# Quantising `w_down` and part of `w_gate` between the steps of attention instead of after it

## The chip, the cores and the metric

One Trainium2 chip, all 8 of its cores. Each core runs the same program on one of the 8 sequences of the batch; no core talks to another. The metric is the device time of the slowest core, in microseconds.

## The reference

One transformer layer in post-norm form, on `x` of 8 x 2048 x 1024. Attention has 16 heads of width 64, and its scores are multiplied by a decay in the distance of the two positions. The feed-forward part quantises its activations and all three weights to FP4 values in blocks of 16 along the last dimension.

```python
scores = einsum('bqhd,bkhd->bhqk', q, k) * scale
scores = scores * exp(-alpha * |i - j|)
attn   = softmax(scores)
x = layernorm(x + (attn @ v) @ Wo.T + bo)

def fp4_quant_dequant(x):            # blocks of 16
    scale = max(max(|xb|) / 6, 1e-12)
    xn = xb / scale
    return GRID[searchsorted(MID, |xn|)] * sign(xn) * scale
def fp4_linear(x, w): return fp4_quant_dequant(x) @ fp4_quant_dequant(w).T

h = silu(fp4_linear(x, w_gate)) * fp4_linear(x, w_up)    # w_gate, w_up: 2816 x 1024
x = layernorm(x + fp4_linear(h, w_down))                 # w_down: 1024 x 2816
```

## The kernel before

There is no scheduler. `Prog` keeps one list of instructions for each engine, filled in the order in which the Python code is run, and each engine works through its own list strictly in that order. `wait` puts a semaphore wait in front of what follows, `do` adds an instruction that raises a semaphore, and `chain` adds one that also waits for everything its own engine has done so far. VectorE raises `sV`, TensorE `sT`, ScalarE `sA`; loads by the SyncE queue raise `dS`.

The work of a core runs in these stages, one after the other:

1. `x` is loaded and transposed, and Q, K and V are projected.
2. **Attention** (the loop at L413). The 8 pairs of heads and 4 blocks of 512 queries make 32 units, and each unit has 16 steps `kt`, one for each 128 keys: 512 steps in all. In a step TensorE computes the scores of both heads of the pair into `ps_s1` and `ps_s2` (L423; two buffers each, so TensorE can be two steps ahead of VectorE), and then, for the same `kt` of the unit before, the products with V and the row sums into `ps_av` and `ps_d` (L397, L404). VectorE multiplies the scores by the decay table `Wd` with two 128x512 instructions (L449), into the ring `SDr1`/`SDr2`. It waits there for all that TensorE was given in this step. After every fourth step ScalarE takes the exponential of the four steps' scores for each head (L461) and writes `PT1`/`PT2`. The ring holds 12 steps, three groups of four. At the end of a unit ScalarE turns the row sums into reciprocals (`recD`, L477 and L479), and VectorE multiplies `ps_av` by them (L484). TensorE's products of the next unit wait for that.
3. The output projection, the residual sum and the first layer norm, whose result goes to `x1_dram`.
4. The normed activations are loaded, quantised and transposed into `x1qT`, in 8 slices.
5. **`w_down`** (loop at L664): 8 rows of 128x2816 are loaded to `wst`, quantised into `wqo`, and stored to `wdq_dram`.
6. **`w_gate` and `w_up`** (loop at L684): 11 chunks each, of 2 rows of 128x1024. A chunk is loaded, quantised, and transposed on TensorE through `emit_pe_tp` (L209: eight groups of two transposes, each evacuated by a VectorE copy, L219) into `wgT` or `wuT`.
7. Gate, up, SiLU and the quantising of `h`, for 16 tiles of tokens; `h` is transposed by DMA and stored.
8. `wdq_dram` is loaded and transposed, and the down projection, the residual sum and the last layer norm follow.

`quant_stages` (L125) quantises a tile in two halves, and each half in three stages. `front` has six VectorE instructions: the maximum of each block (L150), the scale (L153), its reciprocal (L156), the normed values (L157), and two roundings (L159, L165). `mid` has two, a comparison (L172) and a predicated copy (L177). `back` has four (L182, L184, L187, L188). That is 12 for a half and 24 for a tile, all on VectorE and all chained. ScalarE adds a square in `front` (L163) and one in `mid` (L175) for each half.

Of the kernel before, what the change touches and what calls it, by code (L numbers as in the profile page):

```python
# [6 lines left out]
F32 = mybir.dt.float32  # L7
# [8 lines left out]
D = 1024  # L16
# [43 lines left out]
def build_program(debug=False):  # L60
# [17 lines left out]
    wdq_dram = nc.dram_tensor("wdq_scr", [D, I_FF], BF16, kind="Internal").ap()  # L78
    hqT_dram = nc.dram_tensor("hqT_scr", [NTT, 128, I_FF], BF16, kind="Internal").ap()
# [11 lines left out]
    with ExitStack() as es:  # L91
# [29 lines left out]
        junk_t = es.enter_context(nc.sbuf_tensor("junk_t", [128, 256], BF16))  # L121
# [129 lines left out]
        with nc.sbuf_tensor("QT", [128, NCT * T], BF16) as QT, \  # L251
# [121 lines left out]
            with nc.sbuf_tensor("SDr1", [128, 12 * 512], F32) as SDr1, \  # L373
                 nc.sbuf_tensor("SDr2", [128, 12 * 512], F32) as SDr2, \
# [8 lines left out]
                p.wait("tensor", sA, sA_proj)  # L383
                wd_stride = 3968
                units = [(hp, qc) for hp in range(NP) for qc in range(NQC)]
                sd_kt = {0: 0, 1: 0}
                exp_ring = {0: 0, 1: 0, 2: 0}
# [25 lines left out]
                for u in range(len(units) + 1):  # L413
                    if u < len(units):
                        hp, qc = units[u]
                        for kt in range(NTT):
                            b2 = kt % 2
                            r8 = (kt // 4) % 3
# [24 lines left out]
                            s8 = kt % 12  # L443
# [11 lines left out]
                            if kt % 4 == 3:  # L455
# [10 lines left out]
                                exps_grp[(u, g)] = sA.n  # L466
                    if u >= 1:
# [19 lines left out]
                        evac_done[up] = sV.n  # L487
            sV_attn = sV.n
# [123 lines left out]
        if True:  # L612
# [41 lines left out]
            with nc.sbuf_tensor("wgT", [128, NCT * I_FF], BF16) as wgT, \  # L654
# [4 lines left out]
                with nc.sbuf_tensor("wst", [128, 2 * I_FF], F32) as wst, \  # L659
                     nc.sbuf_tensor("wqo", [128, 2 * I_FF], BF16) as wqo:  # L660
                    wd_r = wd_h.rearrange("(r p) i -> p r i", p=128)
                    wdq_r = wdq_dram.rearrange("(r p) i -> p r i", p=128)
                    q_end = {0: 0, 1: 0}
                    for rt in range(8):  # L664
                        par = rt % 2
                        p.wait("sync", sV, q_end[par])
                        p.wait("sync", dS, dS.n)
                        p.do("sync", lambda e, rt=rt, par=par: e.dma_start(
                            out=wst.ap()[:, par * I_FF:(par + 1) * I_FF],
                            in_=wd_r[:, rt, :]), dS, 16)  # L670
                        p.wait("vector", dS, dS.n)
                        p.wait("vector", dWQ[par])
                        emit_quant(wst.ap()[:, par * I_FF:(par + 1) * I_FF], I_FF, qb,
                                   wqo.ap()[:, par * I_FF:(par + 1) * I_FF])
                        q_end[par] = sV.n
                        p.wait("gpsimd", sV, sV.n)
                        p.do("gpsimd", lambda e, rt=rt, par=par: e.dma_start(
                            out=wdq_r[:, rt, :], in_=wqo.ap()[:, par * I_FF:(par + 1) * I_FF]), dWQ[par], 16)
# [5 lines left out]
                    for w_src, wTa, dbgk in ((wg_h, wgTa, "d_wgq"), (wu_h, wuTa, None)):  # L684
                        w_r = w_src.rearrange("(r p) c -> p r c", p=128)
                        for ch in range(11):
                            par = cidx % 2
                            cidx += 1
                            p.wait("sync", sV, q_end[par])
                            p.wait("sync", dS, dS.n)  # L690
                            p.do("sync", lambda e, ch=ch, w_r=w_r, par=par: e.dma_start(
                                out=wst.ap()[:, par * I_FF:par * I_FF + 2 * D].rearrange(
                                    "p (r c) -> p r c", c=D),
                                in_=w_r[:, 2 * ch:2 * ch + 2, :]), dS, 16)
                            p.wait("vector", dS, dS.n)
                            p.wait("vector", sT, wqo_reads[par])
                            p.wait("vector", dWQ[0])
                            p.wait("vector", dWQ[1])
                            wqop = wqo.ap()[:, par * I_FF:par * I_FF + 2 * D]
                            emit_quant(wst.ap()[:, par * I_FF:par * I_FF + 2 * D], 2 * D, qb, wqop)  # L700
# [252 lines left out]
```

How the kernel before makes its waits and increments, by code:

```python
    def wait(self, eng, sem, val=None):  # L42
        v = sem.n if val is None else val
        if v <= 0:
            return
        self.ops[eng].append(lambda e, s=sem.h, v=v: e.wait_ge(s, v))
# [1 line left out]
    def do(self, eng, fn, sem=None, k=1):  # L48
        if sem is not None:
            sem.n += k
            self.ops[eng].append(lambda e, f=fn, s=sem.h, kk=k: f(e).then_inc(s, kk))
        else:
            self.ops[eng].append(fn)
```

## Time and profile before

| what | us |
|---|---|
| median of the timed runs (3241.70 to 3243.77) | 3242.74 |
| the profiled execution's own time | 3252.38 |
| its span on the slowest core (core 2) | 3250.8 |
| spans of the eight cores | 3230.2 to 3250.8 |
| VectorE busy (share of the span) | 2194.5 (68%) |
| TensorE matmuls busy | 1452.6 (45%) |
| ScalarE busy | 969.1 (30%) |

The span is the time from the first to the last instruction on one core; about 1.6 us of the profiled execution lie around it. The profiled execution was some 10 us longer than the median. A busy share is taken over the whole program, whose stages are bound by different things, so it doesn't tell which engine sets the time of a stage; the stages have to be read one by one.

### The profile page before, as it was taken

The page shows a single profiled execution, that of the slowest core. Times are in us where ns is not written, and L with a number is a line of the kernel's source. Part 1 is how long each engine was busy: PE and PEld are TensorE (multiplying, and loading weights), DVE is VectorE, ACT ScalarE, POOL GpSimd, SP SyncE. Part 2 cuts the span into 40 slices and gives each one's busy share as a digit, 9 for nine tenths or more (in the row PEclk, how much of TensorE's full clock was granted, in tenths as well). Part 3 has the DMA queues.
Part 4 walks back from the last instruction along what each step waited for, and adds up shares of the span by engine and source line. Part 5 has one row for each costly group of instructions (what it writes and reads, how often), then busy time and mean ns, then how long its engine had stood idle before and what let it go on. Part 6 is the DMA issues. An engine that isn't in the chain of part 4 may idle for free.

```text
span 3250.8 us, 25238 instructions; the slowest of 8 cores (3230.2 to 3250.8 us)
## 1 busy us (share of the span) xinstructions
PE 1452.6 (45%) x7186; PEld 540.4 (17%) x7186; DVE 2194.5 (68%) x2968; ACT 969.1 (30%) x844; POOL 23.1 (1%) x37
## 2 busy tenths in 40 slices
PE   5777655556555557100000000000046666663298
PEld 2332111111111112000000000000022222221243
DVE  2004766777666754688899788888868888888233
ACT  1214555555555544211112111111112222222022
POOL 0000000000000000000000000000000000000000
PEclk9888888888888878555555555555568888887599
DMA  5110000000000015210222111111100111111344
GB/s 78 26 26 1 1 1 1 1 1 1 1 1 1 1 27 161 84 39 26 81 61 75 48 39 39 39 39 39 39 1 22 39 38 46 39 39 39 115 176 157
DMA packets 88473, 136.95 MB, mean 42 GB/s; under 512 B 59154, under 2 KB 59154, under 8 KB 87314
## 3 DMA queue, kind: packets, MB, share of 16 engines
q1 hardware_dynamic: 73986, 88.66, 9.2%
q0 software_dynamic: 9744, 29.89, 3.9%
q10 hardware_dynamic: 4608, 16.78, 1.3%
q8 instruction: 62, 1.02, 0.1%
q14 instruction: 73, 0.60, 0.1%
HBM read 102.25 MB, written 34.08 MB: 42 GB/s over the span
## 4 chain that ended last, share of the span: by engine, by line
DVE 46%; PE 19%; ACT 16%; issue 11%; DMA 6%; DVEq 1%; SPq 1%; ACTq 0%; POOL 0%; POOLq 0%
ACT PT L461 12%; DVE SDr L449 6%; PE ps_o L850 5%; DVE qc L187 5%; DVE qxn L157 5%; DVE qr L150 5%; PE ps_q L327 4%; DVE qc L177 3%; DVE qm L182 3%; DVE qc L159 3%; DVE qc L184 3%; DVE wqo L188 2%; DVE qm L172 2%; DVE qr L156 2%; PE ps_av L397 2%
## 5 line engine op out<-in xcount | busy, mean ns | idle before, releaser
L449 DVE TENSOR_TENSOR SDr<-ps_s,Wd 128x512 f32<-128x512 f32 x1024 | 640.4, 684 | 311.1 <-PE ps_s L423 220.8
L461 ACT ACTIVATE PT<-SDr 128x2048 bf16<-128x2048 f32 x256 | 474.9, 1902 | 402.9 <-DVE SDr L449 402.9
L163 ACT ACTIVATE qcc<-qc 128x1024 bf16<-128x1024 bf16 (+1 forms) x108 | 129.5, 1199 | 1144.8 <-DVE qc L159 1144.8
L215 PE MATMUL ps_tp<-idn,wqo 128*128 128x128 bf16 x352 | 52.6, 291 | 803.7 <-DVE wqo L188 781.9
L397 PE MATMUL ps_av<-PT,VV 128*64 128x512 bf16 x1024 | 236.1, 453 | 222.4 <-DVE QT L484 222.4
L744 PE MATMUL ps_g<-wgT,x1qT 128*128 128x512 bf16 (+1 forms) x768 | 212.4, 430 | 182.7 <-DVE hbuf L763 182.0
L423 PE MATMUL ps_s<-QT,KT 64*128 64x512 bf16 x1024 | 221.8, 421 | 157.4 <-DVE SDr L449 152.5
L404 PE MATMUL ps_d<-PT,ones 128*64 128x512 bf16 x1024 | 226.9, 434 | 0.0
L750 PE MATMUL ps_u<-wuT,x1qT 128*128 128x512 bf16 (+1 forms) x768 | 185.2, 388 | 0.0
L175 ACT ACTIVATE qcc<-qc 128x1024 bf16<-128x1024 bf16 (+1 forms) x108 | 129.5, 1199 | 125.9 <-DVE qm L172 125.9
L215 PEld LDWEIGHTS ps_tp<-idn,wqo 128*128 128x128 bf16 x352 | 25.7, 108 | 830.5 <-issue 826.0
L187 DVE COPY_PREDICATED qc<-qm,qc 128x1024 bf16<-128x1024 int8 (+1 forms) x108 | 151.9, 1406 | 11.1
L177 DVE COPY_PREDICATED qc<-qm,qc 128x1024 bf16<-128x1024 int8 (+1 forms) x108 | 151.8, 1406 | 11.1
L850 PE MATMUL ps_o<-wdT,hin 128*128 128x512 bf16 x704 | 154.1, 382 | 3.3 <-DMA x1in<-x_scr 3.3
L484 DVE TENSOR_TENSOR QT<-ps_av,recD 128x512 bf16<-128x512 f32 x32 | 22.1, 692 | 179.2 <-ACT recD L479 179.2
L423 PEld LDWEIGHTS ps_s<-QT,KT 64*128 64x128 bf16 x1024 | 63.4, 94 | 429.7 <-issue 429.7
L744 PEld LDWEIGHTS ps_g<-wgT,x1qT 128*128 128x128 bf16 x768 | 77.8, 108 | 303.3 <-issue 260.5
L327 PE MATMUL ps_q<-XT,wbuf 128*128 128x512 bf16 x512 | 115.1, 389 | 18.5 <-DMA wbuf<-wkT 17.8
L397 PEld LDWEIGHTS ps_av<-PT,VV 128*64 128x64 bf16 x1024 | 61.4, 111 | 355.8 <-issue 354.8
L215 PE MATMUL ps_tp<-idn,x1q 128*128 128x128 bf16 x128 | 18.8, 291 | 219.2 <-DVE x1q L188 211.3
L763 DVE TENSOR_TENSOR hbuf<-sg,ps_u 128x512 f32<-128x512 f32 x96 | 61.5, 641 | 68.4 <-ACT sg L757 68.4
L750 PEld LDWEIGHTS ps_u<-wuT,x1qT 128*128 128x128 bf16 x768 | 81.3, 106 | 98.7 <-issue 38.6
(95 smaller groups left out, 1901.1 us busy)
## 6 DMA issues: line engine op xcount, KB each, us to landing
wst<-wd SPq DMA_DIRECT2D x8, 1408.0 KB
wst<-wg SPq DMA_DIRECT2D x11, 1024.0 KB
wst<-wu SPq DMA_DIRECT2D x11, 1024.0 KB
hqT_scr<-hqT POOLq DMA_DIRECT2D x16, 704.0 KB, 3.4
hin<-hqT_scr SPq DMA_DIRECT2D x16, 704.0 KB
xres<-x SPq DMA_DIRECT2D x16, 512.0 KB, 4.5
x_scr<-ra ACTq DMA_DIRECT2D x16, 512.0 KB, 2.7
x1sl<-x_scr SPq DMA_DIRECT2D x8, 1024.0 KB
```

The costliest lines, as they stand in the source:

```text
L150: C(lambda e, d=d: e.tensor_reduce(out=d["r"], in_=d["src3"], axis=AX.X, op=ALU.max, apply_absolute_value=True))
L177: C(lambda e, d=d: e.copy_predicated(out=d["c1"], mask=d["m"], data=d["c2"]))
L187: C(lambda e, d=d: e.copy_predicated(out=d["c1"], mask=d["m"], data=d["c2"]))
L327: p.do("tensor", lambda e, i=i, j=j, q4=q4, g=g: e.matmul(out=psq[:, g, q4 * 512:(q4 + 1) * 512], lhsT=wba[:, i, j * 128:(j + 1) * 128], r ...
L397: p.do("tensor", lambda e, kt=kt, PT=PT, rq0=rq0, h=h: e.matmul(out=ps_av.ap()[rq0:rq0 + 64, :], lhsT=VVa[:, kt, h * 64:(h + 1) * 64], rhs ...
L404: p.do("tensor", lambda e, kt=kt, PT=PT, rq0=rq0: e.matmul(out=ps_d.ap()[rq0:rq0 + 64, :], lhsT=ones64[:, :], rhs=PT.ap()[:, kt * QC:(kt + ...
L423: e.matmul(out=ps.ap()[:, b2 * 512:b2 * 512 + QC], lhsT=KTa[rq0:rq0 + 64, hp, kt * 128:(kt + 1) * 128], rhs=QTa[rq0:rq0 + 64, hp, qc * QC: ...
L449: return e.tensor_tensor(out=SDr.ap()[:, s8 * 512:(s8 + 1) * 512], in0=ps.ap()[:, b2 * 512:b2 * 512 + QC], in1=wd_ap, op=ALU.mult)
L461: e.activation(out=PT.ap()[:, 4 * g * QC:(4 * g + 4) * QC], in_=SDr.ap()[:, r8 * 2048:(r8 + 1) * 2048], func=AF.Exp), sA, 1)
L744: e.matmul(out=ps_g.ap()[:, g * 512:g * 512 + ilen], lhsT=x1qTa[:, i, tt * 128:(tt + 1) * 128], rhs=wgTa[:, i, i0:i0 + ilen], start=(i == ...
L750: e.matmul(out=ps_u.ap()[:, g * 512:g * 512 + ilen], lhsT=x1qTa[:, i, tt * 128:(tt + 1) * 128], rhs=wuTa[:, i, i0:i0 + ilen], start=(i == ...
L850: p.do("tensor", lambda e, it=it, c=c, g=g, hin3=hin3: e.matmul(out=pso[:, g, c * 512:(c + 1) * 512], lhsT=hin3[:, it, :], rhs=wdTa[:, it, ...
```

## The change

The same quantising of `w_down`, and of the first 8 of the 22 rows of `w_gate`, is recorded inside the loop over the attention steps. It is cut into 24 chunks: 16 half rows of `w_down` (128x1408) and 8 rows of `w_gate` (128x1024). Each chunk owns 21 steps in a row; its load, six quantising stages and store come behind the VectorE work of steps 0, 2, 4, 6, 8, 10, 12 and 13 of the 21. A half of a chunk is thus 704 or 512 columns wide. New buffers of their own (`awst`, `awq` and the `aq...` tiles) hold the work, and to make room for them the ring of scores goes from 12 steps to 8. The quantised rows of `w_gate` go to a new scratch `wgq_dram`. Stage 5 is gone; in stage 6 the first four chunks of `w_gate` are loaded from `wgq_dram` straight into `wqo` and only transposed, and the other 18 chunks are as before.

```diff
+    wgq_dram = nc.dram_tensor("wgq_scr", [I_FF, D], BF16, kind="Internal").ap()
...
-            with nc.sbuf_tensor("SDr1", [128, 12 * 512], F32) as SDr1, \
-                 nc.sbuf_tensor("SDr2", [128, 12 * 512], F32) as SDr2, \
+            with nc.sbuf_tensor("SDr1", [128, 8 * 512], F32) as SDr1, \
+                 nc.sbuf_tensor("SDr2", [128, 8 * 512], F32) as SDr2, \
...
+                for rt in range(8):
+                    for hf in range(2):
+                        aw_chunks.append((wd_r2[:, rt, hf * 1408:(hf + 1) * 1408],
+                                          wdq_r2[:, rt, hf * 1408:(hf + 1) * 1408],
+                                          1408))
+                for row in range(8):
+                    aw_chunks.append((wg_r2[:, row, :], wgq_r2[:, row, :], 1024))
...
+                def aw_actions(k):
+                    src, dst, Fk = aw_chunks[k]
+                    stg = quant_stages(awst.ap()[:, :Fk], Fk, aqb, awq.ap()[:, :Fk])
+                    def a_load():
+                        if k >= 1:
+                            p.wait("sync", sV, aw_read[k - 1])
+                        p.wait("sync", dS, dS.n)
+                        p.do("sync", lambda e, src=src, Fk=Fk: e.dma_start(
+                            out=awst.ap()[:, :Fk], in_=src), dS, 16)
+                        aw_load[k] = dS.n
+                    def a_f0():
+                        p.wait("vector", dS, aw_load[k])
+                        stg[0]()
+                    def a_f1():
+                        stg[1]()
+                        aw_read[k] = sV.n
+                    def a_b0():
+                        if k >= 1:
+                            p.wait("vector", dWQ[0], aw_store[k - 1])
+                        stg[4]()
+                    def a_store():
+                        p.wait("gpsimd", sV, sV.n)
+                        p.do("gpsimd", lambda e, dst=dst, Fk=Fk: e.dma_start(
+                            out=dst, in_=awq.ap()[:, :Fk]), dWQ[0], 16)
+                        aw_store[k] = dWQ[0].n
+                    return [a_load, a_f0, a_f1, stg[2], stg[3], a_b0, stg[5],
+                            a_store]
+                for k in range(len(aw_chunks)):
+                    acts = aw_actions(k)
+                    base = k * 21
+                    for oi, off in enumerate((0, 2, 4, 6, 8, 10, 12, 13)):
+                        aw_sched[base + off] = acts[oi]
...
-                            r8 = (kt // 4) % 3
+                            r8 = (kt // 4) % 2
...
-                            s8 = kt % 12
+                            s8 = kt % 8
...
                                 exps_grp[(u, g)] = sA.n
+                            act = aw_sched.get(u * NTT + kt)
+                            if act is not None:
+                                act()
...
-                    for rt in range(8):
...
-                        emit_quant(wst.ap()[:, par * I_FF:(par + 1) * I_FF], I_FF, qb,
-                                   wqo.ap()[:, par * I_FF:(par + 1) * I_FF])
...
+                    for w_src, wTa, preq, dbgk in ((wg_h, wgTa, 4, "d_wgq"),
+                                                   (wu_h, wuTa, 0, None)):
...
+                            if ch < preq:
+                                p.wait("sync", sT, wqo_reads[par])
+                                p.wait("sync", dS, dS.n)
+                                p.do("sync", lambda e, ch=ch, wq3=wq3: e.dma_start(
+                                    out=wq3, in_=wgq_r[:, 2 * ch:2 * ch + 2, :]), dS, 16)
+                                p.wait("tensor", dS, dS.n)
+                            else:
...
```

**VectorE's list, the end of the first unit that has a normalisation.** `SDr` is the scaled scores, `QT` the normed output of the unit before, `aqm`, `aqc`, `aqs` and `awq` the new quantising tiles. Before:

```order
L449 TENSOR_TENSOR SDr<-ps_s,Wd 128x512 [waits sT,sA]
L449 TENSOR_TENSOR SDr<-ps_s,Wd 128x512
L484 TENSOR_TENSOR QT<-ps_av,recD 128x512 [waits sA,sT]
L449 TENSOR_TENSOR SDr<-ps_s,Wd 128x512 [waits sT,sA]
L449 TENSOR_TENSOR SDr<-ps_s,Wd 128x512
```

and now (the line numbers are those of the changed kernel):

```order
L524 TENSOR_TENSOR SDr<-ps_s,Wd 128x512 [waits sT,sA]
L524 TENSOR_TENSOR SDr<-ps_s,Wd 128x512
L183 TENSOR_SCALAR aqm<-aqcc 128x704 [waits dWQa,sA,sV]
L185 TENSOR_SCALAR aqc<-aqxn 128x704 [waits sV]
L188 COPY_PREDICATED aqc<-aqm,aqc 128x704 [waits sV]
L189 TENSOR_TENSOR awq<-aqc,aqs 128x704 [waits sV]
L562 TENSOR_TENSOR QT<-ps_av,recD 128x512 [waits sA,sT]
L524 TENSOR_TENSOR SDr<-ps_s,Wd 128x512 [waits sT,sA]
L524 TENSOR_TENSOR SDr<-ps_s,Wd 128x512
```

Here a `back` stage falls on step 15, between the last scores of the unit and the instruction that waits for `recD`.

**VectorE's list, inside a unit.** Two steps that stood next to each other before,

```order
L449 TENSOR_TENSOR SDr<-ps_s,Wd 128x512 [waits sT]
L449 TENSOR_TENSOR SDr<-ps_s,Wd 128x512
L449 TENSOR_TENSOR SDr<-ps_s,Wd 128x512 [waits sT]
L449 TENSOR_TENSOR SDr<-ps_s,Wd 128x512
```

now have a `front` stage between them; the first one of all also waits for the load (`dS`):

```order
L524 TENSOR_TENSOR SDr<-ps_s,Wd 128x512 [waits sT]
L524 TENSOR_TENSOR SDr<-ps_s,Wd 128x512
L151 TENSOR_REDUCE aqr<-awst 128x44 [waits dS,sV]
L154 TENSOR_SCALAR aqs<-aqr 128x44 [waits sV]
L157 RECIPROCAL aqr<-aqs 128x44 [waits sV]
L158 TENSOR_TENSOR aqxn<-awst,aqr 128x704 [waits sV]
L160 TENSOR_SCALAR aqc<-aqxn 128x704 [waits sV]
L166 TENSOR_SCALAR aqc<-aqxn 128x704 [waits sV]
L524 TENSOR_TENSOR SDr<-ps_s,Wd 128x512 [waits sT]
L524 TENSOR_TENSOR SDr<-ps_s,Wd 128x512
```

The next scores can't start until the six instructions are done.

**SyncE's queue behind the loads of the activations.** Before it held the loads of `wd`, `wg` and `wu`:

```order
L668 DMA wst<-wd 128x2816 [waits sV,dS]
L668 DMA wst<-wd 128x2816 [waits dS]
L668 DMA wst<-wd 128x2816 [waits sV,dS] x6
L691 DMA wst<-wg 128x2x1024 [waits sV,dS] x11
L691 DMA wst<-wu 128x2x1024 [waits sV,dS] x11
```

and now:

```order
L759 DMA wqo<-wgq_scr 128x2x1024 [waits sV,dWQa,dS]
L759 DMA wqo<-wgq_scr 128x2x1024 [waits dS]
L759 DMA wqo<-wgq_scr 128x2x1024 [waits sT,dS] x2
L765 DMA wst<-wg 128x2x1024 [waits dS] x2
L765 DMA wst<-wg 128x2x1024 [waits sV,dS] x5
L765 DMA wst<-wu 128x2x1024 [waits sV,dS] x11
```

Eight loads of `wd` have gone and four of the eleven chunks of `wg` come from the scratch; each load still waits for the one before it (`dS`).

## Rows read from the trace of the kernel before

**Rows 1.** Page part 2: busy tenths and granted clock, slices of 81.3 us

```profile
DVE  2004766777666754688899788888868888888233
...
PEclk9888888888888878555555555555568888887599
```

**Rows 2.** By stage: PE, PEld, DVE, ACT, POOL busy, clock, DMA, GB/s

```profile
274.89:1207.50 932.61, 551.85 (x3070) 144.94 (x3068) 662.40 (x1056) 514.15 (x320) 0.00 (x0) 0.82 0.00 1
...
1549.90:1804.66 254.76, 0.00 (x0) 0.00 (x0) 216.11 (x193) 44.05 (x32) 4.30 (x8) 0.50 0.24 76
1804.66:2404.80 600.14, 51.95 (x348) 25.45 (x348) 499.73 (x701) 93.02 (x88) 0.00 (x0) 0.50 0.10 35
```

**Rows 3.** VectorE's waits in the attention stage: us, times, longest

```profile
DVE QT L484 <- ACT recD L479: 179.2, 32, 10.4
DVE SDr L449 <- PE ps_d L404: 69.1, 107, 1.6
DVE SDr L449 <- ACT PT L461: 4.4, 2, 4.0
```

**Rows 4.** Timeline at a unit boundary: start, duration, instruction, idle before

```profile
699.50 1.89 ACT L461 ACTIVATE PT<-SDr 128x2048 bf16<-128x2048 f32 x1
701.48 0.60 ACT L477 ACTIVATE recD<-ps_d 128x512 f32<-128x512 f32 x1
...
702.97 0.69 DVE L484 TENSOR_TENSOR QT<-ps_av,recD 128x512 bf16<-128x512 f32 x1 [5.44 <-ACT recD L479]
...
705.16 1.29 DVE L449 TENSOR_TENSOR SDr<-ps_s,Wd 128x512 f32<-128x512 f32 x2 [1.50 <-PE ps_d L404]
...
706.71 1.29 DVE L449 TENSOR_TENSOR SDr<-ps_s,Wd 128x512 f32<-128x512 f32 x2 [0.26 <-PE ps_d L404]
...
708.75 17.91 DVE L449 TENSOR_TENSOR SDr<-ps_s,Wd 128x512 f32<-128x512 f32 x28 [0.75 <-PE ps_s L423]
```

**Rows 5.** TensorE, two short stretches there: length, busy, clock, DMA

```profile
704.80:705.60 0.80, 0.80 (x6) 0.50 0.00 0
710.40:711.20 0.80, 0.73 (x6) 1.00 0.00 0
```

**Rows 6.** Groups by shape: busy us, mean ns of one, idle before

```profile
L187 DVE COPY_PREDICATED qc<-qm,qc 128x1408 bf16<-128x1408 int8 x48 | 78.1, 1628 | 4.9
...
L187 DVE COPY_PREDICATED qc<-qm,qc 128x1024 bf16<-128x1024 int8 x60 | 73.7, 1228 | 6.2
...
L163 ACT ACTIVATE qcc<-qc 128x1408 bf16<-128x1408 bf16 x48 | 66.1, 1377 | 496.9 <-DVE qc L159 496.9
...
L157 DVE TENSOR_TENSOR qxn<-wst,qr 128x1024 f32<-128x1024 f32 x44 | 53.9, 1226 | 5.0 <-DVE qr L156 0.5
...
L159 DVE TENSOR_SCALAR qc<-qxn 128x1408 bf16<-128x1408 f32 x48 | 42.9, 894 | 5.1
...
L159 DVE TENSOR_SCALAR qc<-qxn 128x1024 bf16<-128x1024 f32 x60 | 41.6, 694 | 6.4
...
L156 DVE RECIPROCAL qr<-qs 128x88 f32<-128x88 f32 x48 | 33.7, 703 | 5.0
L156 DVE RECIPROCAL qr<-qs 128x64 f32<-128x64 f32 x60 | 33.2, 553 | 6.2
...
L157 DVE TENSOR_TENSOR qxn<-wst,qr 128x1408 f32<-128x1408 f32 x16 | 26.0, 1626 | 1.7
...
L153 DVE TENSOR_SCALAR qs<-qr 128x64 f32<-128x64 f32 x60 | 11.7, 195 | 6.7 <-DVE qr L150 0.5
```

**Rows 7.** Timeline: first instructions of two successive rows of `wd`

```profile
1557.36 1.62 DVE L150 TENSOR_REDUCE qr<-wst 128x88 f32<-128x1408 f32 x1 [7.46 <-DMA wst<-wd]
...
1586.89 1.62 DVE L150 TENSOR_REDUCE qr<-wst 128x88 f32<-128x1408 f32 x1
```

**Rows 8.** Chain that ended last: two loads (start us, us)

```profile
1326.29 5.68 DMA x1sl<-x_scr
...
3047.30 4.41 DMA wdq_sb<-wdq_scr
```

More of the change, by code:

```diff
@@ L120, in build_program @@
         small = es.enter_context(nc.sbuf_tensor("small", [128, 16], F32))
-        junk_t = es.enter_context(nc.sbuf_tensor("junk_t", [128, 256], BF16))
+        junk_t = es.enter_context(nc.sbuf_tensor("junk_t", [128, 16], BF16))
         idn = es.enter_context(nc.sbuf_tensor("idn", [128, 128], BF16))
@@ L383, in build_program @@
                 p.wait("tensor", sA, sA_proj)
+                aq_es = ExitStack()
+                aq_sb = lambda n, sh, dt: aq_es.enter_context(nc.sbuf_tensor(n, sh, dt))
+                awst = aq_sb("awst", [128, 1408], F32)
+                awq = aq_sb("awq", [128, 1408], BF16)
+                aqxn = aq_sb("aqxn", [128, 1408], F32)
+                aqc1 = aq_sb("aqc1", [128, 1408], BF16)
+                aqc2 = aq_sb("aqc2", [128, 1408], BF16)
+                aqcc = aq_sb("aqcc", [128, 1408], BF16)
@@ new lines, in build_program @@
+                aqm = aq_sb("aqm", [128, 1408], I8)
+                aqr = aq_sb("aqr", [128, 88], F32)
+                aqs = aq_sb("aqs", [128, 88], F32)
+                aqb = {"r": aqr.ap(), "s": aqs.ap(), "xn": aqxn.ap(),
+                       "c1": aqc1.ap(), "c2": aqc2.ap(), "cc": aqcc.ap(),
+                       "m": aqm.ap()}
+                wd_r2 = wd_h.rearrange("(r p) i -> p r i", p=128)
+                wdq_r2 = wdq_dram.rearrange("(r p) i -> p r i", p=128)
+                wg_r2 = wg_h.rearrange("(r p) c -> p r c", p=128)
@@ new lines, in build_program @@
+                aw_load = {}
+                aw_read = {}
+                aw_store = {}
+                p.wait("sync", dG, dG.n)
+                p.wait("sync", sT, sT.n)
+                p.wait("sync", sV, sV.n)
+                aw_sched = {}
+                def aw_actions(k):
[25 more added lines that the diff above has]
+                            a_store]
@@ L660, in build_program @@
                      nc.sbuf_tensor("wqo", [128, 2 * I_FF], BF16) as wqo:
-                    wd_r = wd_h.rearrange("(r p) i -> p r i", p=128)
-                    wdq_r = wdq_dram.rearrange("(r p) i -> p r i", p=128)
+                    p.wait("sync", dWQ[0])
                     q_end = {0: 0, 1: 0}
-                    for rt in range(8):
[L665 to L672, printed above, removed]
-                        emit_quant(wst.ap()[:, par * I_FF:(par + 1) * I_FF], I_FF, qb,
-                                   wqo.ap()[:, par * I_FF:(par + 1) * I_FF])
[L675 to L678, printed above, removed]
                     cidx = 0
@@ L683, in build_program @@
                     wT_done = 0
-                    for w_src, wTa, dbgk in ((wg_h, wgTa, "d_wgq"), (wu_h, wuTa, None)):
+                    wgq_r = wgq_dram.rearrange("(r p) c -> p r c", p=128)
+                    for w_src, wTa, preq, dbgk in ((wg_h, wgTa, 4, "d_wgq"),
+                                                   (wu_h, wuTa, 0, None)):
                         w_r = w_src.rearrange("(r p) c -> p r c", p=128)
@@ L688, in build_program @@
                             cidx += 1
[L689 to L695, printed above, removed]
@@ L709, in build_program @@
                                 p.wait("gpsimd", sV, sV.n)
+                                p.wait("gpsimd", dS, dS.n)
                                 p.do("gpsimd", lambda e, ch=ch, dbgk=dbgk, wq3=wq3: e.dma_start(
```

23 lines of the change are left out of this document (16 added, 7 removed).

## The prediction

> **What bounds the kernel now.** I read the views in this order: the slices of the page, the same times by stage, VectorE's waits in attention, the timeline of one unit boundary, and the groups of instructions by shape.
>
> The slices show VectorE at 6 to 9 tenths in most of the program, and TensorE's granted clock at half (5 tenths) from slice 17 to 29, where it has little to do [rows 1]. By stage, the quantising of `w_down` takes 254.8 us with 216.1 us of VectorE work and no matmul at all, and the stage of `w_gate` and `w_up` takes 600.1 us with 499.7 us of VectorE work [rows 2]. The gaps there are the short pauses between chained instructions, so both stages are bound by VectorE. Attention takes 932.6 us with 662.4 us of VectorE work [rows 2]: VectorE idles for 270 us of it, which looks like room for work from elsewhere.
>
> The waits tell where this room lies. 179.2 us are one wait in each of 32 units, for `recD`; 69.1 us are waits for TensorE before a score [rows 3]. The timeline shows the shape of it: behind the last scores ScalarE does two exponentials (1.89 us the one shown), 0.60 us and as much again for the reciprocal, and VectorE idles 5.44 us; then it idles 1.50 us for TensorE, and after two steps it runs 28 score instructions in 17.91 us, one step in 1.28 us, with no gap [rows 4]. So in 13 or 14 of a unit's 16 steps VectorE is the bound itself, and work put between these steps is paid in full.
>
> **What the new instructions cost.** The trace has them at halves of 1408 and 1024 columns [rows 6]. Three of the twelve run like L157 (1626 and 1226 ns; the maximum and the last product are of that kind), two are predicated copies (1628 and 1228), five are like L159 (894 and 694), one is the reciprocal (703 and 553), and L153 takes 0.2 us. A half is 3 x 1.626 + 2 x 1.628 + 5 x 0.894 + 0.703 + 0.2 = 13.51 us at 1408 columns and 10.35 us at 1024: 8.23 ns a column, and some 1.9 us that don't depend on the width. On that line a half of 704 columns takes 7.72 us and one of 512 takes 6.14 us. The pauses come on top: two rows of `w_down` start 29.53 us apart [rows 7], of which 2 x 13.51 = 27.02 are work; 2.5 us for 24 instructions, 0.105 us each. A chunk of `w_down` then costs 15.44 + 2.5 = 17.94 us, 16 of them 287 us, and one of `w_gate` 12.28 + 2.5 = 14.78 us, 8 of them 118 us. **Added: 405 us**, because halves half as wide pay the fixed part twice as often: `w_down` alone took 8 x 29.53 = 236 us before.
>
> The pauses are a place where the Trainium skill says otherwise. "VectorE: DVE Perf Modes", section "The DRAIN you can't avoid", has it that the semaphore between chained instructions costs nothing extra. By this rule the 24 chunks would cost 405 - 60 = 345 us. The rows speak against it: the 2.5 us in 29.53 are there where nothing else runs, and score instructions with no wait between them follow each other at 0.64 us.
>
> **What of it is hidden.** Counting 21 x k + offset over the 24 chunks, 9 of the 144 quantising stages fall on a step 15, in front of the wait for `recD`: 2 `front`, 3 `mid`, 4 `back`. At 704 columns a `front` is 4.1 us, a `mid` 1.6, a `back` 3.3 (the pieces above with their pauses); at 512 a `mid` is 1.3 and a `back` 2.7. A `back` is hidden whole by the 5.44 us: 2 x 3.3 + 2 x 2.7 = 12 us. `front` and `mid` also put a square into ScalarE's list ahead of the reciprocal; 1.377 us at 1408 columns [rows 6], so 0.7 to 0.9 here, which delays `recD` by 0.8 to 0.9. What stays hidden is 2 x 3.2 + 2 x 0.7 + 0.5 = 8 us. **Hidden: 20 us.** The ring of two groups does no harm: a pair of exponentials takes 3.8 us, and VectorE fills a group in four steps, 5.1 us or more, before it needs that pair's space. It even takes away the 4.4 us in which the second unit waited for the exponential of the first one's last group [rows 3]: **4 us saved**.
>
> **TensorE's clock.** After the idle time at a unit's end the granted clock is 0.50, which is 1.2 GHz, and later in the unit 1.00, 2.4 GHz [rows 5]. At the low level a step is paced by TensorE, at 706.71 - 705.16 = 1.55 us instead of 1.28 [rows 4]. Taking 31 first waits of 1.50 us from the 69.1 leaves 22.6 us, which is what cold steps cost now. In the changed kernel TensorE idles behind each quantising stage, so I expect it at 1.2 GHz there. That costs nothing while stages follow every second step: two steps and the shortest stage take 2.56 + 1.3 = 3.9 us of VectorE and 3.1 to 3.3 us of a cold TensorE. Eleven steps follow the last stage of a chunk without one; TensorE is ahead by two, and nine run free; as at a unit's start I take 0.7 us (22.6 / 32) for each of 24 chunks, 17 us, and drop half of the old 22.6, since about half of the unit starts lie between stages. **Net 6 us lost**, with bounds of -22 (never cold outside) and +50 (all 24 x 9 free steps cold, 216 x 0.33 = 71 us, less 22).
>
> Loads are not in the way: the load of a chunk may start when `front` of the one before is done, some 17 steps ahead, and the DMA engines are idle in attention (0.00 [rows 2]). The stores on POOL's queue have nothing behind them until attention ends. `junk_t` has no part in it.
>
> **Attention in all:** 405 - 20 - 4 + 6 = **387 us longer**.
>
> **What goes.** From 1549.9 to 2404.8 us, 854.9 us lie between the activations' last transpose and the gate matmuls [rows 2]. Instead of that: four loads of 512 KB, each behind the one before. A load of 704 KB took 4.41 us and one of 1024 KB 5.68 [rows 8], so I take 4.3 us each, 17.2 us; the bounds are 3 and 5.7, thus -5 and +6 us. The eight transpose groups of a chunk (about 4 us) fit beside the next load. Then the first `wst` load shows, about 6 us. Then 18 chunks at 600.14 / 22 = 27.28 us [rows 2], 491 us. Sum 514 us, so **341 us are saved**. The three later stages have the same instructions as before.
>
> **Sum:** 387 - 341 = +46 us. The profiled execution took 3252.4 us, so it would be 3298; its distance to the median of the timed runs, some 10 us, isn't the change's, and 3242.7 + 46 = **3289 us**, 1.4% more. Two per cent, about what a measurement of this kernel can tell from no change, is 65 us, so 3178 to 3308 counts as the same.
>
> **Rivals.**
> - *A cold TensorE takes over as the bound (slower).* If its clock stays at 1.2 GHz through all of attention, the free steps are paced by it and the clock term is +50 instead of +6: 3289 + 44 = 3333 us. It decides if more than about 60 of the 216 free steps beyond those in the sum are cold (19 / 0.33). For it: the low clock at each unit's start, and the average of 0.82. Against it: at the low clock TensorE is busy for nearly all of a free step (0.80 of 0.80 [rows 5]), and in this kernel it came back to 2.4 GHz within three such steps. The Trainium skill ("TensorE: Matmul & The Clock Gate", section "HAM oscillation") names this pattern: bursts of matmuls parted by waits each start cold again.
> - *VectorE waits for ScalarE (slower).* A `mid` needs the square of the `front` four steps before, and that square may stand behind a pair of exponentials (3.8 us) that itself waits for TensorE. If each `mid` lost 0.6 us, 48 x 0.6 = 29 us: 3318 us. Against: four steps last 5.1 us without the stages.
> - *The stage's idle time takes the work (faster).* If VectorE's 270 us in attention could be filled but for the 46.5 us at unit starts, 224 us would be hidden: 405 - 224 - 341, some -160 us, 3083 us. For it: the busy share of 71%. Against it: 135 of the 144 stages don't stand in front of the long wait, and VectorE works in order.
> - *The pauses vanish in attention (same).* 60 us less: 3229 us.
>
> **How the numbers follow.** Forecast 0.69, cold TensorE 0.12, ScalarE 0.09, idle time filled 0.04, no pauses 0.06. The forecast's own spread (the clock's bounds, the loads, 0.02 us on 576 pauses is 12 us) puts about 0.10 of its 0.69 above 3308. Slower by over 2%: 0.10 + 0.12 + 0.06 of ScalarE's = 0.28. Faster by over 2%: 0.04. Same: 0.68. The range leaves out the filled idle time and the far ends of the rest: 3245 to 3332 us.
>
> **What would show it.** Right: attention about 1320 us long in the windows, with VectorE busy some 1007 us (662 + 345 of instructions without their pauses); the wait for `recD` down from 179 to about 160 us; chunks of `w_down` whose instructions last 0.89 us (L158) and 0.53 us (L160); gate matmuls some 46 us later than before; hardly any wait for the DMA of `awst`. Wrong: attention much shorter than 1290 us would mean that the stages were hidden; over 1350 us with waits for `ps_d` of 100 us or more would mean a cold TensorE; waits of `aqm` for `aqcc` on ScalarE would be the second rival; a stage of four passes much over 23 us would mean that the loads were mis-sized.

## The result and the profile after

The changed kernel took 3273.18 us (median of 20 runs) against 3246.02 us for the kernel before (median of 19): a ratio of 1.0088, with a 95% interval of 1.0060 to 1.0117. That is 0.9% slower, 27 us between the two medians, within the 2% that count as no change. The forecast was 3289 us, with a range of 3245 to 3332 and a chance of 0.68 for "the same".

The profiled execution took 3296.77 us, with a span of 3295.2 us on core 7. Two cores of it, 6 and 7, came out of the projections 25 to 35 us late at a lower clock (0.76 instead of 0.92 over the same 210 us), which no other core shows. That lies in front of the change, and run 2 below, which has the projections and attention of the kernel before, shows the same on two of its cores; so everything below is read stage by stage.

First the page's busy tenths and granted clock after the change:

```profile
DVE  2002877777777777777358878888877888888323
...
PEclk9777557676666666666785555555559889887599
```

They are the counterpart of [rows 1]: VectorE is at 7 tenths from the third slice of attention to its end, where it went between 6 and 7 before, and the clock there has come down from 8 to 5, 6 and 7.

The stages, in the columns of [rows 2]: attention, the activations' quantising, the four chunks that are only transposed, and the other 18 chunks of weights.

```profile
307.72:1609.90 1302.18, 678.45 (x3070) 152.66 (x3068) 997.06 (x1632) 585.20 (x416) 13.02 (x24) 0.65 0.05 19
...
1724.30:1948.70 224.40, 18.70 (x128) 9.39 (x128) 181.59 (x256) 33.84 (x32) 0.00 (x0) 0.50 0.11 38
1948.70:1969.50 20.80, 9.57 (x64) 4.47 (x64) 8.53 (x33) 0.00 (x0) 0.00 (x0) 0.50 0.46 152
1969.50:2458.50 489.00, 42.19 (x288) 21.06 (x288) 408.28 (x575) 76.13 (x72) 0.00 (x0) 0.50 0.11 37
```

Attention takes 1302.2 us instead of 932.6, 369.6 more. Behind the activations, 20.8 + 489.0 = 509.8 us stand in the place of 854.9, 345.1 less. The two leave 24.5 us, and the medians of the runs show 27.

VectorE's waits in attention, the counterpart of [rows 3]:

```profile
DVE QT L562 <- ACT recD L557: 158.8, 32, 10.6
DVE SDr L524 <- PE ps_d L479: 76.8, 108, 1.6
...
DVE SDr L524 <- ACT PT L536: 1.3, 4, 0.4
```

The wait for `recD` has lost 20.4 us, the waits for TensorE have gained 7.7, and the wait for the exponentials is down by 3.1 us. So VectorE's idle time in attention has hardly been touched: the work went on top. The timeline shows how. Between steps (start, duration, instruction, idle time before it):

```profile
735.02 2.48 DVE L524 TENSOR_TENSOR SDr<-ps_s,Wd 128x512 f32<-128x512 f32 x4 [0.39 <-issue]
...
737.61 0.89 DVE L151 TENSOR_REDUCE aqr<-awst 128x44 f32<-128x704 f32 x1
...
741.05 0.53 DVE L166 TENSOR_SCALAR aqc<-aqxn 128x704 bf16<-128x704 f32 x1
...
741.50 2.47 DVE L524 TENSOR_TENSOR SDr<-ps_s,Wd 128x512 f32<-128x512 f32 x4
...
744.07 0.89 DVE L151 TENSOR_REDUCE aqr<-awst 128x44 f32<-128x704 f32 x1
```

and at a unit's end, with ScalarE's two instructions for `recD`:

```profile
717.59 0.89 DVE L189 TENSOR_TENSOR awq<-aqc,aqs 128x704 bf16<-128x704 bf16 x1
719.17 0.60 ACT L555 ACTIVATE recD<-ps_d 128x512 f32<-128x512 f32 x1
719.86 0.63 ACT L557 ACTIVATE recD<-recD 128x512 f32<-128x512 f32 x1
720.66 0.69 DVE L562 TENSOR_TENSOR QT<-ps_av,recD 128x512 bf16<-128x512 f32 x1 [2.18 <-ACT recD L557]
```

Two steps of scores end at 737.50, a `front` stage of a 704-column half fills VectorE until 741.58, and two more steps follow: the stage has moved them by 4.00 us, all of it paid. At the unit's end a `back` stage ends at 718.48, inside the wait, which is 2.18 us long instead of 5.44 [rows 4]; that one was hidden.

The new shapes in the groups by shape:

```profile
L178 DVE COPY_PREDICATED aqc<-aqm,aqc 128x704 bf16<-128x704 int8 x32 | 28.6, 895 | 3.3
...
L158 DVE TENSOR_TENSOR aqxn<-awst,aqr 128x704 f32<-128x704 f32 x32 | 28.5, 892 | 3.3
...
L160 DVE TENSOR_SCALAR aqc<-aqxn 128x704 bf16<-128x704 f32 x32 | 16.9, 527 | 3.4
```

They are what the straight line through the two widths of [rows 6] gives for 704 columns: 0.89 to 0.90 us and 0.53.

### The profile page after: what moved, and what is told of

It is laid out like the page before. It is cut to its first block, busy times and chain, and to the rows that moved or that the text cites. A ratio compares the mean times of both kernels' runs of the same rounds, so it can differ in the third digit from the quotient of the medians.

```text
span 3295.2 us, 26073 instructions; the slowest of 8 cores (3258.1 to 3295.2 us)
## 1 busy us (share of the span) xinstructions
PE 1601.8 (49%) x7186; PEld 553.1 (17%) x7186; DVE 2228.5 (68%) x3256; ACT 979.6 (30%) x892; POOL 31.3 (1%) x53
## 4 chain that ended last, share of the span: by engine, by line
DVE 50%; PE 20%; issue 14%; ACT 8%; DMA 5%; DVEq 1%; SPq 1%; ACTq 0%; POOL 0%; POOLq 0%
DVE SDr L524 13%; ACT PT L536 5%; PE ps_o L922 5%; PE ps_q L328 4%; DVE qc L188 4%; DVE qxn L158 4%; DVE qr L151 4%; PE ps_q L348 2%; PE ps_av L472 2%; DVE qc L178 2%; PE ps_tp L216 2%; DVE qc L185 2%; DVE qm L183 2%; DVE qc L160 2%; DVE qm L173 2%
## 5 line engine op out<-in xcount | busy, mean ns | idle before, releaser
L498 PE MATMUL ps_s<-QT,KT 64*128 64x512 bf16 x1024 | 269.1, 514 | 377.7 <-DVE SDr L524 372.1
L472 PE MATMUL ps_av<-PT,VV 128*64 128x512 bf16 x1024 | 281.1, 541 | 245.0 <-DVE QT L562 245.0
L164 ACT ACTIVATE qcc<-qc 128x1024 bf16<-128x1024 bf16 (+1 forms) x84 | 99.1, 1179 | 882.0 <-DVE qc L160 882.0
L479 PE MATMUL ps_d<-PT,ones 128*64 128x512 bf16 x1024 | 276.1, 530 | 0.0
L822 PE MATMUL ps_u<-wuT,x1qT 128*128 128x512 bf16 (+1 forms) x768 | 177.5, 376 | 0.0
L328 PE MATMUL ps_q<-XT,wbuf 128*128 128x512 bf16 x512 | 138.3, 445 | 16.7 <-DMA wbuf<-wkT 16.0
L562 DVE TENSOR_TENSOR QT<-ps_av,recD 128x512 bf16<-128x512 f32 x32 | 22.1, 691 | 158.8 <-ACT recD L557 158.8
L176 ACT ACTIVATE qcc<-qc 128x1024 bf16<-128x1024 bf16 (+1 forms) x84 | 99.1, 1179 | 102.1 <-DVE qm L173 102.1
L178 DVE COPY_PREDICATED qc<-qm,qc 128x1024 bf16<-128x1024 int8 (+1 forms) x84 | 115.9, 1380 | 9.0 <-DVE qm L173 0.5
L188 DVE COPY_PREDICATED qc<-qm,qc 128x1024 bf16<-128x1024 int8 (+1 forms) x84 | 115.9, 1380 | 8.6
L822 PEld LDWEIGHTS ps_u<-wuT,x1qT 128*128 128x128 bf16 x768 | 79.3, 103 | 91.9 <-issue 26.9
```

What stands on the lines that cost most here:

```text
L178: C(lambda e, d=d: e.copy_predicated(out=d["c1"], mask=d["m"], data=d["c2"]))
L188: C(lambda e, d=d: e.copy_predicated(out=d["c1"], mask=d["m"], data=d["c2"]))
L328: p.do("tensor", lambda e, i=i, j=j, q4=q4, g=g: e.matmul(out=psq[:, g, q4 * 512:(q4 + 1) * 512], lhsT=wba[:, i, j * 128:(j + 1) * 128], r ...
L472: p.do("tensor", lambda e, kt=kt, PT=PT, rq0=rq0, h=h: e.matmul(out=ps_av.ap()[rq0:rq0 + 64, :], lhsT=VVa[:, kt, h * 64:(h + 1) * 64], rhs ...
L479: p.do("tensor", lambda e, kt=kt, PT=PT, rq0=rq0: e.matmul(out=ps_d.ap()[rq0:rq0 + 64, :], lhsT=ones64[:, :], rhs=PT.ap()[:, kt * QC:(kt + ...
L498: e.matmul(out=ps.ap()[:, b2 * 512:b2 * 512 + QC], lhsT=KTa[rq0:rq0 + 64, hp, kt * 128:(kt + 1) * 128], rhs=QTa[rq0:rq0 + 64, hp, qc * QC: ...
```

## The experiments

Where runs are compared by stage, attention is counted on each core from its first score instruction to the end of its last normalising one, and the weights from the activations' last transpose to the first gate matmul. By that count the eight cores of the kernel before have 932 to 933 and 853 to 857 us, those of the changed one 1301 to 1304 and 511 to 513.

**1. Only what the change removes.** The 144 stages are left out; loads, stores, the short ring and the shorter stage of weights stay (the load of a chunk now waits for the store of the one before it). The run leaves the quantising of `w_down` and of 8 rows of `w_gate` undone.

```diff
-                            if act is not None:
+                            if act is not None and (u * NTT + kt) % 21 in (0, 13):
...
-                            out=dst, in_=awq.ap()[:, :Fk]), dWQ[0], 16)
+                            out=dst, in_=awst.ap()[:, :Fk]), dWQ[0], 16)
```

> The changed kernel with the 144 quantising stages left out of attention; the 24 loads and stores stay, the store now writes the loaded values unquantised, so the weights of w_down and of the first 8 rows of w_gate are not quantised in this run. All that is left of the change is what it removes. Theory that the stages cost 369 us of VectorE's line in attention (what the trace shows) and that loads, stores and the shorter ring cost nothing there: attention back at 929 to 933 us and 3273 - 370 = 2903 us. Rival that part of the 369 us belongs to the loads, the stores or the ring of two groups: attention stays above 940 us.

Attention took 928 to 929 us on six cores and 936 and 938 us on two, where the waits for TensorE were 77 and 79 us instead of 69. This run's window of attention on core 0, in the columns of [rows 2]:

```profile
275.90:1204.70 928.80, 551.94 (x3070) 144.81 (x3068) 662.45 (x1056) 514.11 (x320) 12.83 (x24) 0.82 0.10 26
```

and VectorE's waits on its slowest core:

```profile
DVE QT L563 <- ACT recD L558: 179.6, 32, 10.4
...
DVE SDr L525 <- PE ps_d L480: 68.8, 106, 1.6
```

The waits are those of [rows 3] but for the wait for the exponentials, which went from 4.4 to 0.8 us, and the stage is 3.8 us shorter than before the change: the shorter ring saves what was worked out (4 us), and loads and stores cost nothing. On core 0 the stages cost 1301.5 - 928.8 = 373 us. The timed runs of this kernel scattered from 2899 to 2971 us (median 2928); the lowest two and the stages agree with 2903.

**2. Narrow halves where the work stood before.** Each row of `w_down` is quantised in two pieces of 1408 columns, after attention.

```diff
-                        emit_quant(wst.ap()[:, par * I_FF:(par + 1) * I_FF], I_FF, qb,
-                                   wqo.ap()[:, par * I_FF:(par + 1) * I_FF])
+                        for hf in range(2):
+                            c0 = par * I_FF + hf * 1408
+                            emit_quant(wst.ap()[:, c0:c0 + 1408], 1408, qb,
+                                       wqo.ap()[:, c0:c0 + 1408])
```

> The kernel before, with each row of w_down quantised as two pieces of 1408 columns, thus in halves of 704, where it stands, after attention. Theory that a half has a fixed part of some 1.9 us and 12 pauses of 0.105 us whatever its width: 8 x (2 x 17.94 - 29.53) = 51 us more, 3246 + 51 = 3297. Rival that the width of a half makes no difference and the narrow halves have no part in the result: 3246 within 5 us.

Measured were 3297.62 us (ratio 1.0130, 1.0037 to 1.0223), and 905 to 907 us of weights instead of 853 to 857: some 51 us, as worked out. The window of that stage on core 0:

```profile
1540.40:2444.70 904.30, 52.22 (x353) 25.76 (x354) 747.02 (x1088) 143.54 (x152) 4.30 (x8) 0.50 0.13 45
```

So cutting the halves to 704 columns would by itself have cost nearly twice the whole loss.

**3. A wait behind each stage.** The score instruction behind a stage waits for the stage's last instruction.

```diff
                             if act is not None:
                                 act()
+                                if (u * NTT + kt) % 21 in (2, 4, 6, 8, 10, 12):
+                                    p.wait("vector", sV, sV.n)
```

> The changed kernel in which the score instruction behind each of the 144 stages waits for the stage's last instruction, as chained instructions do. Theory that a stage is cheaper in attention than in its own stage because what follows it is not chained (in the trace the next score starts 0.08 us before the stage's last instruction ends, where a chained one starts 0.10 us after it): 144 x 0.18 = 26 us more, about 3299. Rival that a semaphore between two VectorE instructions costs nothing extra: 3273 within 3 us.

Measured were 3319.06 us, and 1347 to 1349 us of attention: 47 us more, not 26 and not nothing. The timeline at one stage's end:

```profile
759.31 0.89 DVE L189 TENSOR_TENSOR awq<-aqc,aqs 128x704 bf16<-128x704 bf16 x1
760.45 2.48 DVE L524 TENSOR_TENSOR SDr<-ps_s,Wd 128x512 f32<-128x512 f32 x4 [0.24 <-DVE awq L189]
```

The stage's last instruction ends at 760.20, and the score starts 0.24 us later; in the changed kernel, `aqc` at 741.05 ends at 741.58 and the score starts at 741.50. That is 0.32 us for each of the 135 stages that have a score behind them, 44 us; the waits for TensorE grew by 2.5 us besides (79.3 against 76.8). The direction of the forecast was right and its size was not. In VectorE's list the wait for the stage's own count now stands in front, and those for TensorE and ScalarE behind it. They have long been met, and still each adds 0.07 us: with two of them the score starts 0.24 us after the stage (the median of 132 places), with one, in the three places where the ring isn't yet waited for, 0.17 us. Where the own count is the last of the waits, it takes 0.10 to 0.11 us however many stand in front of it, as at `aqm` (L183), which has three. So what costs is a wait still to be handled when the last open one is met.

**4. Stages at every third step.**

```diff
-                    for oi, off in enumerate((0, 2, 4, 6, 8, 10, 12, 13)):
+                    for oi, off in enumerate((0, 2, 5, 8, 11, 14, 17, 18)):
```

> The changed kernel with the six quantising stages of a chunk behind steps 2, 5, 8, 11, 14 and 17 of its 21 instead of 2, 4, 6, 8, 10 and 12. The same instructions, and again 9 of 144 stages on a step 15. Theory that TensorE's low clock costs wherever a third step follows a stage (a cold step is paced at 1.55 us, a VectorE step at 1.24 to 1.28): some 0.3 us at each of 144 stages, less the 17 us that free steps cost already, so 20 to 35 us more than the changed kernel's 3273, and waits of the scores for ps_d of 100 us or more instead of 77. Rival that VectorE's own work is all that counts: 3273 within 5 us.

Measured were 3336.60 us (1.0284, 1.0225 to 1.0344) with attention at 1354 to 1358 us, some 53 us more than in the changed kernel. The instructions are the same, and 9 of the 144 stages stand on a step 15 again; the wait for `recD` is 160.4 us (158.8 in the changed kernel). The timed runs lie between 3321 and 3357 us. First VectorE's wait for TensorE in this run, then its timeline behind one stage:

```profile
DVE SDr L524 <- PE ps_d L479: 126.4, 182, 1.7
```

and

```profile
723.73 2.48 DVE L524 TENSOR_TENSOR SDr<-ps_s,Wd 128x512 f32<-128x512 f32 x4
...
725.15 0.61 PE L498 MATMUL ps_s<-QT,KT 64*128 64x512 bf16 x2 [4.32 <-DVE SDr L524]
...
726.94 1.29 DVE L524 TENSOR_TENSOR SDr<-ps_s,Wd 128x512 f32<-128x512 f32 x2 [0.74 <-PE ps_d L479]
```

Waits for TensorE went from 76.8 to 126.4 us, which is most of it. The third step behind a stage finds TensorE at its low level (a pair of score matmuls takes 0.61 us, at the high level 0.39) and waits 0.74 us, more than the 0.3 that were expected. Such third steps waited 92 times, 64 us in all, where the changed kernel has 18 times and 13 us. At the high level the step's six matmuls take 0.95 us (708.15 to 709.10 in the kernel before); started at 725.15 they would have ended at 726.10 by that estimate, before VectorE was free at 726.21. So the stages' place decides even where none of them is hidden: at every second step TensorE is always ahead, at every third it is not.

**5. Work only where VectorE waits.** Ten chunks of `w_down`, five of the six stages of each at unit ends, nothing of `w_gate`.

```diff
+                    u0 = 1 + 3 * k
+                    aw_sched.setdefault(u0 * NTT, []).append(load)
+                    aw_hole[u0] = [f0]
+                    aw_hole[u0 + 1] = [f1, m0]
+                    aw_hole[u0 + 2] = [m1, b0]
+                    aw_sched.setdefault((u0 + 3) * NTT + 5, []).extend([b1, store])
...
                         recd_done[up] = sA.n
+                        for act in aw_hole.get(u, ()):
+                            act()
                         p.wait("vector", sA, sA.n)
```

> Only 5 of the 8 rows of w_down are quantised in attention, as 10 chunks of 1408 columns; of each chunk five of six stages stand right in front of VectorE's wait for recD at the ends of three successive units (4.0, 5.6 and 4.8 us of work in a wait of 5.44 us), behind recD in ScalarE's list, and the sixth (3.2 us) behind step 5 of the unit after. No row of w_gate is moved; rows 5 to 7 of w_down are quantised after attention as before. Theory that work is hidden there and only there: 5 x 29.5 = 148 us saved, 10 x 3.2 = 32 us paid, some 2 us of overflow: 3246 - 114 = 3132 us, and the wait for recD down from 179 to about 30 us. Rival that the wait only moves (recD or TensorE comes later when VectorE is busy in it): the wait stays over 100 us and the time over 3200.

Measured were 3173.83 us (0.9773, 0.9752 to 0.9794): faster than both kernels, but by 72 us and not 114. The timeline of a unit's end shows why:

```profile
701.94 0.53 DVE L166 TENSOR_SCALAR aqc<-aqxn 128x704 bf16<-128x704 f32 x1
...
703.03 0.63 ACT L558 ACTIVATE recD<-recD 128x512 f32<-128x512 f32 x1
703.76 0.79 ACT L164 ACTIVATE aqcc<-aqc 128x704 bf16<-128x704 bf16 x1
704.72 0.69 DVE L565 TENSOR_TENSOR QT<-ps_av,recD 128x512 bf16<-128x512 f32 x1 [2.25 <-ACT aqcc L164]
```

`recD` is done at 703.66, but the normalising instruction starts at 704.72, behind the square of the stage (`aqcc`). Its wait is written as ScalarE's count at that point of the program, and the squares had been counted in.

**6. The same with that wait on `recD` alone.**

```diff
-                        p.wait("vector", sA, sA.n)
+                        p.wait("vector", sA, recd_done[up])
                         p.wait("vector", sT, sT.n)
```

> The earlier run with 10 chunks at unit ends, with one wait changed: the instruction that normalises (QT) waits for ScalarE's count at recD instead of its count at that point of the program, which also took in the squares of the stages placed there (in the trace of the earlier run it starts behind ScalarE's aqcc, not behind recD). Theory that the missing 42 us of the earlier run were 0.8 to 1.5 us of such waits at each of 30 unit ends: 3174 - 32 = 3142 us. Rival that VectorE's and ScalarE's work at the unit end slow each other: 3174 within 5 us.

The timeline at a unit's end of this run:

```profile
713.93 0.63 ACT L558 ACTIVATE recD<-recD 128x512 f32<-128x512 f32 x1
714.10 0.89 DVE L178 COPY_PREDICATED aqc<-aqm,aqc 128x704 bf16<-128x704 int8 x1
714.65 0.79 ACT L164 ACTIVATE aqcc<-aqc 128x704 bf16<-128x704 bf16 x1
714.91 0.68 DVE L565 TENSOR_TENSOR QT<-ps_av,recD 128x512 bf16<-128x512 f32 x1
```

Now it starts when VectorE is free, beside the square. Attention went from 1008 to 973 us, 35 less, and the waits for `recD` are 36.5 us in all. The timed runs (3150.0, ratio 0.9677, 0.9603 to 0.9751) scatter from 3133 to 3164; the stage and the profiled span (3131.0 us, 42 less than in the run before) say that the wait was the cause. In the changed kernel this mistake costs nothing: there the stage on a step 15 is recorded before `recD`, so that ScalarE's count at the normalising instruction is that of `recD`. What its five `front` and `mid` stages on a step 15 do cost is the place of their square in ScalarE's list, ahead of the reciprocal, as the prediction had it:

```profile
793.92 0.79 ACT L164 ACTIVATE aqcc<-aqc 128x704 bf16<-128x704 bf16 x1
794.80 0.60 ACT L555 ACTIVATE recD<-ps_d 128x512 f32<-128x512 f32 x1
```

**7. All six stages at unit ends.**

```diff
-                    aw_hole[u0] = [f0]
+                    aw_hole.setdefault(u0, []).append(f0)
...
-                    aw_sched.setdefault((u0 + 3) * NTT + 5, []).extend([b1, store])
+                    aw_hole.setdefault(u0 + 3, []).extend([b1, store])
```

> As the run before it, and the sixth stage of each chunk (3.2 us) stands at a unit end too, in front of the first stage of the next chunk; 7.2 us of work then stand in a wait of 5.44 us at 9 unit ends. Theory: 1.8 us of overflow instead of 3.2 us paid and about 0.7 us of cold TensorE behind the stage, 10 x 2.1 = 20 us less than the run before it, 3122 us. Rival that work over the length of the wait costs more than its own length, since all of TensorE's next unit starts late: no gain.

It came to 3140.0 us (0.9617, 0.9533 to 0.9701) with runs from 3109 to 3175, and attention to 944 to 945 us, 28 less than in 6 where 20 were expected. As the scatter was as wide as the gain, it was timed again:

> The run with 10 chunks and all six stages at unit ends once more, for its time: its profile had spans of 3092 to 3108 us, its timed runs scattered from 3109 to 3175. Theory, by the stages of its profile (attention 945 us against 932.6, the weights 704 against 854): 3246 + 12 - 150 = 3108 us. Rival that the scatter belongs to this kernel: a median over 3130 again.

3109.91 us against 3246.53 for the kernel before, a ratio of 0.9583 (0.9538 to 0.9628): 4.2% faster. Its windows of attention and of the weights on core 1:

```profile
275.30:1220.90 945.60, 550.31 (x3070) 145.13 (x3068) 816.89 (x1296) 545.77 (x360) 5.46 (x10) 0.82 0.04 12
1563.80:2268.30 704.50, 51.37 (x353) 25.85 (x354) 580.69 (x776) 109.52 (x100) 1.61 (x3) 0.50 0.12 42
```

Attention is 945.6 us with 154.5 us of quantising instructions in it, for 13 us more than before (VectorE is busy for 816.9 us of it instead of 662.4), and 17 us more than in run 1, which has the same short ring and no stages; the weights take 705 us instead of 854. This version beats both kernels.

**8. All 24 chunks with the unit ends filled first,** with the wait as it was and then with the wait on `recD`.

```diff
+                aw_total = sum(c for _, _, _, c in aw_seq)
...
+                    while j < len(aw_seq) and aw_seq[j][3] <= room and s < goal + 1.0:
...
+                    aw_hole[u] = [g[2] for g in grp]
```

> All 24 chunks in attention as in the changed kernel, but the stages are dealt out so that one to three of them stand in front of the wait for recD at each of the 31 unit ends; summed, some 124 us of work stand there (counting no more than 5.44 us for each end) where the changed kernel hides 20. Theory that the stages' place alone decides: 3273 - 104 = 3169 us. Rival that the stages' amount decides and their place does not: 3273 within 10 us.

> The earlier run with all 24 chunks and the unit ends filled, now with the normalising instruction waiting for recD alone. That run gained 34 of the 104 us expected; its attention took 1270 us. Theory that two things had eaten the rest: waits for squares at the unit ends, as in the runs with 10 chunks (some 25 to 30 us, which go now), and a colder TensorE, whose waits (ps_d) had grown from 77 to 112 us and stay: attention some 1242 us, 3210 us in all, and ps_d still above 100 us. Rival that the squares had no part in it: 3239 within 5 us.

The first took 3239.16 us, the second 3213.60 (0.9879, 0.9838 to 0.9921), with attention at 1267 to 1272 and 1242 to 1247 us. VectorE's waits in the second:

```profile
DVE SDr L558 <- PE ps_d L513: 112.3, 181, 1.6
...
DVE QT L597 <- ACT recD L590: 52.7, 25, 10.7
```

So the first gained 34 of the 104 us that were expected, the second 60. The squares cost 26 us, as expected. The waits for `recD` are 52.7 us, 106 less than in the changed kernel: the ends took in what had been counted. But the waits for TensorE are 112.3 us, 35.5 more. They grew where run 4 would have it: at the third step behind a stage, where stages are more than two steps apart, this trace has 54 waits and 39 us, that of the changed kernel 18 and 13 us, while the waits behind the unit starts are alike (9 us). Even with the ends filled, moving all 24 chunks is 104 us worse than moving ten: the other stages are paid, and paid at the price of narrow halves.

## Why the prediction was right

The change was forecast as a loss of 46 us that counts as "the same"; it was one of 27. The mechanism held, term by term, but the two traces differ by 24.5 us, little more than half of the sum.

**The bound.** That attention is bound by VectorE between steps, and that its idle time is at the unit ends, holds. Leaving the stages out gives back all they cost (1), and 154.5 us of such work at the unit ends cost 17 us where it costs its own length elsewhere (7). The rival "the stage's idle time takes the work" has fallen for this change: 20.4 us were hidden of 405. It was right that the room is there; only place decides who gets it.

**What the instructions cost.** The durations were right to 0.01 us. VectorE's busy time went from 662.4 to 997.1 us, 334.7 more and not 345, because the score behind a stage starts 0.08 us before the stage's last instruction ends: 135 x 0.084 = 11.3 us. The forecast added up durations and had no term for this overlap. That narrow halves cost 51 us was measured (2).

**The pauses** were the term that was mis-sized. Forecast: 576 x 0.105 = 60 us. In the trace: 369.6 - 334.7 + 20.4 - 7.7 + 3.1 = 50.7 us. The pauses themselves are all there, 63 us: 432 between a stage's own instructions (737.61 + 0.89 to the next at 738.60 is 0.10) and 144 between the last score and the stage (737.50 to 737.61). What the forecast missed is what they replace. It read the 28 score instructions of [rows 4] as standing without a gap, but between steps there are small gaps of up to 0.15 us, 15.2 us in all of attention before. The steps behind a stage find their scores ready and run without them: four score instructions in 2.47 us, 0.62 each, where 28 took 17.91, 0.64 each. Only 4.8 us of small gaps are left, 10 us less. The overlap (10 us) and this term (9 us) are what the forecast of 387 us had too much; the waits for TensorE and the exponentials (2.6 us more than forecast) take it to 17. By the rule that a semaphore costs nothing extra (the Trainium skill, "VectorE: DVE Perf Modes", section "The DRAIN you can't avoid") the wait behind each stage in run 3 should have cost nothing. It cost 47 us, so the rule doesn't fit here, and the measurement decides.

**What is hidden** was 20 us forecast, 20.4 measured. The single ends bear it out: the wait for `recD` is 1.9 to 2.3 us behind a `front` instead of 5.44, 4.7 to 4.8 behind a `mid` and 2.2 to 2.8 behind a `back`. **The ring** was 4 us forecast, 3.8 in run 1.

**TensorE's clock.** Forecast +6 us, measured +7.7 in the waits for `ps_d`. That this is so near is in part luck, since both of its parts were larger: the waits in the steps behind a chunk's last stage are 25 us (17 forecast), and those behind the first step of a unit went from 25 to 9 us, 16 less (11 forecast); gaps over 0.15 us are counted here as waits. The granted clock in attention fell from 0.82 to 0.65, part of the way to the 0.50 of the rival. The section "HAM oscillation" of "TensorE: Matmul & The Clock Gate" in the Trainium skill has bursts of matmuls parted by waits start cold each time, and this trace agrees where a `front` stage keeps TensorE waiting:

```profile
737.65 0.39 PE L498 MATMUL ps_s<-QT,KT 64*128 64x512 bf16 x2 [0.25 <-DVE SDr L524]
...
742.92 0.61 PE L498 MATMUL ps_s<-QT,KT 64*128 64x512 bf16 x2 [4.32 <-DVE SDr L524]
```

But with stages at every second step TensorE is two steps ahead even so. One step further apart it was not, and at the same average clock (0.65) the waits for it were 50 us longer (4): the rival's mechanism is real, and this change missed it by its spacing.

**What goes.** 341 us forecast, 345.1 measured. Of the 4 us between them 3 are the loads, 3.6 us for 512 KB instead of 4.3 (four of them from 1948.85 to 1963.22), and the 18 chunks took 489 us instead of 491. Two loads in the chain that ended last:

```profile
1948.85 3.62 DMA wqo<-wgq_scr
...
1963.22 5.82 DMA wst<-wg
```

The first `wst` load took 5.82 us (6 forecast). The two terms, 17 us too much in attention and 4 too little behind it, make the 46 us forecast out of the 24.5 that the two traces differ by.

**VectorE waits for ScalarE,** the second rival, didn't happen: between stages the trace has no wait for `aqcc`. In run 5 and the first of run 8 it did at the unit ends, through one wait that was written too wide.

## What to carry to other kernels

Idle time is a place in an engine's list, not a share: work goes into it only if it stands directly in front of the instruction that waits, fits the wait's length, and is hidden whole only if that instruction's wait names only what it needs. Work that costs an engine a fixed part for each piece gets dearer when it is cut to fit, so move only as much as is hidden: 10 chunks at the right places gained 4.2%, 24 chunks with the right places filled first 1.2%, and 24 chunks at arbitrary ones lost 0.9%. When work is put between a producer and a consumer, the distance between the pieces matters as well, since it decides whether the other engine, at its lower clock, is still ahead.

## What the runs showed that was not expected

- What a wait costs VectorE depends on its place: an instruction whose last wait is the open one starts 0.10 us after it is met, one with a further, long met wait behind that 0.17 us, one with two 0.24 us (run 3).
- A VectorE instruction that waits for nothing still open starts 0.08 us before the one in front of it ends (741.50 against 741.58).
- Stages at every third step instead of every second cost 53 us of attention with the same instructions (run 4).
- In the profiled execution of the changed kernel two of the eight cores were granted a clock of 0.76 in the projections where the others had 0.92 or 0.93, and began attention up to 35 us late. In run 2 two cores began it 35 us late too.
